# Query projection written transposed, with Wo loads and spare groups placed anew, in an attention and feed-forward kernel on one Trainium2 core

## What is computed

```python
H, D = 32, 32                                   # heads, head size; Hd = 1024; 4 x 512 = 2048 tokens
xn = layernorm(x)
q = (xn @ Wq.T + bq).reshape(B, S, H, D)        # k and v likewise
scores = einsum('bshd,bsgd->bshg', q, k) / sqrt(D)
scores = where(scores > 0.001, scores, -inf)
attn = softmax(scores)
a = einsum('bshg,bsgd->bshd', attn, v).reshape(B, S, Hd) @ Wo.T + bo
f = (silu(xn @ Wg.T) * (xn @ Wu.T)) @ Wd.T      # Wg, Wu: 3584 x 1024, Wd: 1024 x 3584, int4 x scale
out = x + a + f
```

## Time and profile before

| | |
|---|---|
| Median of 3 runs | 2017.5 us (2017.4 to 2018.03) |
| The profiled execution | 2018.38 us, of which the span (first to last instruction) is 2016.6 us |
| PE busy | 1975.8 us, 98% of the span |
| DVE busy | 1613.4 us, 80% |
| ACT busy | 1183.5 us, 59% |
| POOL busy | 1368.3 us, 68% |
| Granted PE clock, mean | 0.996 of full speed |
| DMA engines, mean busy share of the first 13 of 40 slices | 6 to 9 tenths |

### The profile page before, as it was taken

How to read it: one execution, slowest core, us unless ns; L and a number is a source line. 1 busy time by engine, 2 the same in 40 slices (tenths; PEclk the granted TensorE clock), 3 DMA queues, 4 the chain that set the end, 5 groups by cost and what they waited for, 6 DMA issues and landing times.

```text
span 2016.6 us, 36122 instructions
## 1 busy us (share of the span) xinstructions
PE 1975.8 (98%) x10368; PEld 948.6 (47%) x10368; DVE 1613.4 (80%) x1747; ACT 1183.5 (59%) x1934; POOL 1368.3 (68%) x782
## 2 busy tenths in 40 slices
PE   7999999999998999899999999999999999999997
PEld 5555555555554444344444444444444444444444
DVE  6778788887864100799999999999999999999997
ACT  4566666666755212566656666566665666666663
POOL 1455555555562000588889888898888988889898
PEclk9999999999999999999999999999999999999999
DMA  9686776777767552212212122121221212212136
GB/s 304 156 182 161 178 179 157 183 177 165 178 146 204 134 202 63 52 48 57 79 47 50 49 59 77 47 51 48 60 75 47 52 47 62 74 47 52 47 110 250
DMA packets 398869, 219.51 MB, mean 109 GB/s; under 512 B 335984, under 2 KB 372848, under 8 KB 396784
## 3 DMA queue, kind: packets, MB, share of 16 engines
q1 hardware_dynamic: 398832, 219.02, 41.6%
HBM read 96.29 MB, written 41.94 MB: 69 GB/s over the span
## 4 chain that ended last, share of the span: by engine, by line
PE 88%; DVE 6%; issue 3%; POOL 1%; ACT 1%; DMA 0%; DVEq 0%; SPq 0%; ACTq 0%; POOLq 0%
PE banks L710 34%; PE banks L554 24%; PE banks L735 16%; PE banks L652 8%; DVE lower L1211 5%; PE banks L570 1%; PE banks L603 1%; PE banks L587 1%; PE banks L538 1%; POOL acc L1311 1%; DVE wt L1085 0%; PE banks L768 0%; DMA lower<-in_L_attn_Wo_dram 0%; PE banks L633 0%; DMA x_tile<-in_L_attn_x_dram 0%
## 5 line engine op out<-in xcount | busy, mean ns | idle before, releaser
L710 PE MATMUL banks<-xt,lower 128*128 128x512 f16 x3584 | 855.4, 379 | 12.0 <-DVE lower L1211 6.8
L1311 POOL TENSOR_TENSOR acc<-acc,lower 128x1024 f32<-128x1024 f32 x326 | 766.8, 2364 | 130.0 <-ACT lower L1006 130.0
L1006 ACT ACTIVATE lower<-banks,down_scale 128x512 f32<-128x512 f32 x652 | 412.8, 684 | 366.9 <-PE banks L735 287.8
L1211 DVE SCALAR_TENSOR_TENSOR lower<-banks,gate_scale,lower 128x1024 f32<-128x1024 f32 x386 | 472.8, 1277 | 147.8 <-PE banks L710 147.5
L710 PEld LDWEIGHTS banks<-xt,lower 128*128 128x128 f16 x3584 | 344.1, 98 | 454.6 <-DVE lower L1211 67.6
L554 PE MATMUL banks<-wt,xt_tile 128*128 128x512 f16 x2304 | 527.5, 379 | 0.0
L1211 DVE SCALAR_TENSOR_TENSOR lower<-banks,up_scale,lower 128x1024 f32<-128x1024 f32 x388 | 475.4, 1278 | 30.9 <-PE banks L710 27.1
L735 PE MATMUL banks<-lower 128*128 (+1 forms) x1792 | 458.8, 379 | 1.0 <-ACT lower L1006 0.6
L1269 POOL TENSOR_TENSOR stacks<-unit,stacks 128x512 f16<-128x512 f32 x192 | 236.9, 1259 | 276.4 <-ACT stacks L830 276.4
L554 PEld LDWEIGHTS banks<-wt,xt_tile 128*128 (+1 forms) x2304 | 218.0, 98 | 228.3
L735 PEld LDWEIGHTS banks<-lower 128*128 (+1 forms) x1792 | 171.0, 98 | 217.6 <-ACT lower L1006 11.2
(11 more groups left out here) (60 smaller groups left out, 1285.4 us busy)
## 6 DMA issues: line engine op xcount, KB each, us to landing
v_scratch<-stacks SPq DMA_DIRECT2D x16, 1024.0 KB, 3.9
lower<-in_L_ffn_gate_q_dram SPq DMA_DIRECT2D x28, 512.0 KB, 3.7
lower<-in_L_ffn_up_q_dram SPq DMA_DIRECT2D x28, 512.0 KB, 4.4
lower<-in_L_ffn_down_q_dram SPq DMA_DIRECT2D x28, 512.0 KB, 3.9
x_tile<-in_L_attn_x_dram SPq DMA_DIRECT2D x16, 512.0 KB, 3.8
xt_scratch<-xt_tile SPq DMA_DIRECT2D x16, 512.0 KB, 3.2
ctx_scratch<-ctx_parts SPq DMA_DIRECT2D x64, 128.0 KB, 2.1
lower<-ctx_scratch SPq DMA_DIRECT2D x4, 2048.0 KB, 8.5
```

What stands on the lines that cost most here:

```text
L710: last = mm(psum[:, 2 * (slot % 3) + c, :], gu_t[:, mat, g, :], xt[:, (2 * half + c) * CT:(2 * half + c + 1) * CT, part, g, :], start=(par ...
L1006: run(down_tmp[:, buffer, c * BANK:(c + 1) * BANK], psum[:, 6 + c, :], ACT.Copy, scale=scale)\
L1211: v.scalar_tensor_tensor(out=acc_of[:, half, :], in0=gu_pair(slot % 3), scalar=scale[:, :, :].rearrange("p t k -> p (t k)")[:, bass.ds(t * ...
L1311: g.tensor_tensor(acc[:, half, ho, :], acc[:, half, ho, :], down_tmp[:, buffer, :], ALU.add).then_inc(down_added, 1)
```

## The change

Three things are changed.

**Queries.** In units 0 and 1 `project` swaps the operands: a block of Wq is the stationary side and the 128 tokens are the 128 columns that stream. A step of these units is now 24 matmuls of 128 columns (8 blocks of the hidden size times 3 products) instead of 6 of 512, and the queries leave PE already transposed, features on the partitions. The bias becomes one number per partition (`bias_q`). ACT and POOL write one high and one low part, in a strided order, into the new tile `q_parts` (one instruction each per unit instead of two). The turns R0 to R3, their four copies and `ident16` are gone. Instead `move_queries` copies, behind step 11, blocks of 32 rows by 1024 from `q_parts` to their places in `turned[Q]`: four high blocks by DVE, four low blocks by ACT. Behind step 15 `double_queries` has ACT issue two DMAs that copy each 32-row half to the 32 rows beside it. The scores wait for these two DMAs and for the moves. The order of the heads in a block of scores changes with it (`block_of`).

**Wo.** Four blocks of Wo are loaded ahead: blocks 0 and 1 as soon as unit 1 of tile 15 is done, then context 0, then blocks 2 and 3 into the place of `ctx_b` after unit 3. In the opening the first projections wait for as many weight rows as they use.

**Spare groups.** `SPARE` of feed-forward tile 0 takes groups 4, 7, 10, 13, 20, 23, 26, 29 instead of 4, 5, 10, 11, 20, 21, 26, 27.

```diff
-        STEPS = [["S0"], ["S1"], ["S2"], ["S3"], ["X"], [], [], [], [], [], [], [], [], ["R0"],
-                 ["R1"], ["R2"], ["R3", "V0"], ["V1"], [], ["V2"], ["V3"], [], [], []]
+        STEPS = [["S0"], ["S1"], ["S2"], ["S3"], ["X"], [], [], [], [], [], [], [], [], [],
+                 [], [], ["V0"], ["V1"], [], ["V2"], ["V3"], [], [], []]
+        MOVE_AT, DOUBLE_AT = 11, 15
...
+        MOVED_BY = (((HI, 0), (HI, 1), (HI, 2), (HI, 3)), ((LO, 0), (LO, 1), (LO, 2), (LO, 3)))
+        def move_views(part, j):
+            dst = turned[2 * part * DH:(2 * part + 1) * DH, Q, :].rearrange("d (t j o) -> d t j o", j=TG, o=KT)
+            return dst[:, :, j, :], q_parts[j * DH:(j + 1) * DH, part, :].rearrange("d (t o) -> d t o", o=KT)
+        def queries_split(eng, i):
+            eng.wait_ge(unit_lo, i * 6 + (2 * Q + 2))
+            wait_pos(eng, s_done, i * 4)
...
-        SPARE = ((4, 5, 10, 11, 20, 21, 26, 27), (8, 9))
+        SPARE = ((4, 7, 10, 13, 20, 23, 26, 29), (8, 9))
...
+                if u // 2 == Q:
+                    ks, to = range(KT), psum[:, u % 2, (s % 4) * P:(s % 4 + 1) * P]
...
+                        if u // 2 == Q:
+                            last = mm(to, wt[:, Q, wp, k, s * P:(s + 1) * P], xs, start=start, stop=stop)
+                        else:
+                            last = mm(to, xs, wt[:, u // 2, wp, k, (u % 2) * BANK:(u % 2 + 1) * BANK],
+                                      start=start, stop=stop)
...
-                    pe.wait_ge(batch_out[0], j + 1)
-                    pe.wait_ge(batch_out[1], j * 3 + 3)
+                    pe.wait_ge(q_doubled, j * 32 + 32)
+                    pe.wait_ge(q_moved[0], j * 4 + 4)
+                    pe.wait_ge(q_moved[1], j * 4 + 4)
...
+            def double_queries(i):
+                act.wait_ge(q_moved[0], i * 4 + 4)
+                act.wait_ge(q_moved[1], i * 4 + 4)
+                for part in (HI, LO):
+                    at = 2 * part * DH
+                    act.dma_start(turned[at + DH:at + 2 * DH, Q, :], turned[at:at + DH, Q, :]).then_inc(q_doubled, 16)
...
             def load_wo(n):
-                if n >= 2:
+                if n in (4, 5):
+                    sp.wait_ge(wo_turned, 2 * (n - 3))
+                elif n > 5:
                     sp.wait_ge(wo_turned, 2 * (n - 1))
...
+                if ends(i):
+                    sp.wait_ge(unit_done, 6 * (TT - 1) + 2)
+                    load_wo(0)
+                    load_wo(1)
...
+                if ends(i):
+                    sp.wait_ge(ctx_stored, 64 * 2 * CT)
+                    load_context(0)
+                    sp.wait_ge(unit_done, 6 * (TT - 1) + 4)
+                    load_wo(2)
+                    load_wo(3)
```

More of the change, by code:

```diff
@@ L79, in build @@
         ident32 = sb(whole, "ident32", [P, P], F32)
-        ident16 = sb(whole, "ident16", [P, P], F16)
         bias_o = sb(whole, "bias_o", [P, KT], F32)
@@ L170, in build @@
         k_turned = [sem(f"k_turned{k}") for k in range(2)]
+        q_moved = [sem(f"q_moved_{name}") for name in ("dve", "act")]
+        q_doubled = sem("q_doubled")
         v_stored = sem("v_stored")
@@ L192, in build @@
         xt_loaded = sem("xt_loaded")
-        wo_loaded = [sem(f"wo_loaded{k}") for k in range(2)]
+        wo_loaded = [sem(f"wo_loaded{k}") for k in range(KT)]
         wo_turned = sem("wo_turned")
@@ L824, in unit_part @@
                 if u // 2 == Q:
-                    wait_pos(act, batch_done, i * 4)
-                else:
-                    wait_pos(act, k_turned[u % 2] if u // 2 == K else v_stored, i * 16)
+                    wait_pos(act, q_moved[0], i * 4)
+                    run(query_view(u, HI), query_unit(u), ACT.Copy).then_inc(unit_hi, 1)
+                    return
+                wait_pos(act, k_turned[u % 2] if u // 2 == K else v_stored, i * 16)
                 dst, src = stack_view(u, HI), unit_view(u)
@@ L831, in unit_part, with move_queries @@
                 last.then_inc(unit_hi, 1)
-            def batch_copy(j, m):
-                act.wait_ge(batch_done, j * 4 + (m + 1))
-                dst = batch_dest(act, j, m)
-                run(dst, batch_source(m), ACT.Copy).then_inc(batch_out[0], 1)
+            def move_queries(i):
+                queries_split(act, i)
+                for part, j in MOVED_BY[1]:
+                    dst, src = move_views(part, j)
+                    run(dst, src, ACT.Copy).then_inc(q_moved[1], 1)
+            def double_queries(i):
[4 more added lines that the diff above has]
+                    act.dma_start(turned[at + DH:at + 2 * DH, Q, :], turned[at:at + DH, Q, :]).then_inc(q_doubled, 16)
             def scores_out(j, k):
@@ L897, in tile_2 @@
                             x_part(i + 1)
-                        elif kind == "R" and n == 2:
-                            batch_copy(i, n)
                         elif kind == "S":
@@ L912, in tile_2 @@
                         unit_part(i, s // 4)
+                    if s == MOVE_AT and projects(i):
+                        move_queries(i)
+                    if s == DOUBLE_AT and projects(i):
+                        double_queries(i)
             def first_quarter(s):
@@ L965, in spare_copy @@
                 act.wait_ge(gu_done, units_made(t, GU_SLOT[idx]))
-                if g == 5:
+                if t == 0 and g >= 5:
                     dst = spare_b
@@ L1095, in unit_copy, with move_queries @@
                 wait_pos(dve, unit_lo, i * 6 + (u - 1))
-                v.scalar_tensor_tensor(out=unit32[:, u % 2, :], in0=psum[:, u % 2, :], scalar=W_UNSCALE,
-                                       in1=bias_qkv[:, u // 2, (u % 2) * BANK:(u % 2 + 1) * BANK],
-                                       op0=ALU.mult, op1=ALU.add).then_inc(unit_copied, 1)
-            def batch_copy(j, m):
-                dve.wait_ge(batch_done, j * 4 + (m + 1))
-                dst = batch_dest(dve, j, m)
-                v.tensor_copy(dst, batch_source(m)).then_inc(batch_out[1], 1)
+                out, src = unit32[:, u % 2, :], psum[:, u % 2, :]
+                if u // 2 == Q:
+                    out, src = out.rearrange("p (o t) -> p o t", t=P), src.rearrange("p (o t) -> p o t", t=P)
+                    bias = bias_q[:, 4 * u:4 * u + 4].rearrange("p (o t) -> p o t", t=1).broadcast_to((P, 4, P))
+                else:
+                    bias = bias_kv[:, u // 2 - 1, (u % 2) * BANK:(u % 2 + 1) * BANK]
+                v.scalar_tensor_tensor(out=out, in0=src, scalar=W_UNSCALE, in1=bias, op0=ALU.mult, op1=ALU.add)\
+                    .then_inc(unit_copied, 1)
+            def move_queries(i):
+                queries_split(dve, i)
+                for part, j in MOVED_BY[0]:
+                    dst, src = move_views(part, j)
+                    v.tensor_copy(dst, src).then_inc(q_moved[0], 1)
             def over_heads(ap):
@@ L1179, in first_quarter @@
                     unit_copy(0, 5)
[L1180 to L1181 removed]
+                if s == MOVES_0:
+                    move_queries(0)
             def second_x(w):
@@ L1514, in tile_2 @@
                 if not projects(i):
-                    for n in range(3, KT):
+                    for n in range(4, KT):
                         load_wo(n)
```

127 lines of the change are left out of this document (53 added, 74 removed).

## The result

The kernel after takes 2042.8 us (2040.6 to 2046.7), the kernel before 2017.45 us beside it: ratio 1.0127, 95% interval 1.0115 to 1.0139. The forecast was 2003.5. The profiled execution of after takes 2040.63 us, its span 2038.8; the span before was 2016.6, so 22.2 us are to be found.

A forecast was written before the change was run, and what follows sets the result against it. It took PE's own work as the bound. Tiles -5.3, opening -1.0, Wo -5.7 and spare groups -2.0 sum to -14.0 from the profiled 2018.38, 2004.4; the median is 0.9 lower: 2003.5 us, range 1983 to 2016.

The forecast's parts named there:

- V2's wait: In each tile PE waits at V2 for ACT's path to the low part of V0: 1.1 us, bounds 0 and 3.3.
- the doubling: Two DMAs of 256 KB behind step 15, claimed hidden by over 8 us of PE work: no cost in the tile.
- middle case: V2 waits 1.5 to 2.6 us in each tile, around no change: 2010 to 2026 us, chance 0.11.
- three signs of being wrong: V2 starts without idle; PE waits at S0 for K or doubled rows; the gap between short matmuls exceeds 60 ns.
- PE's work: In a tile, 32 turns removed, Q steps 0.32 us dearer at 55.6 ns per short matmul: net -1.46 us, 34.99 a tile.
- Rival 3: Short Q matmuls on PE don't sustain 55.6 ns; at 81 ns the total would be about 2064 us; chance 0.03.
- rival 1: V2 does not wait, so the full gain comes: tile 34.99 us, total 1987 us; chance 0.26.
- POOL's relief: Fewer POOL instructions beside DVE's softmax steps give back 1.5 us of 2.49, so ACT's split of the probabilities starts earlier.
- Moves: ACT's four moves between unit 2 and unit 3, ahead of V0's context, take 3.8 us, bounds 3.6 and 4.2.
- The two issues: ACT's two doubling DMA issues, put beside unit 3 at no cost; 0.74 us if they hold ACT up.
- Rival 2: ACT becomes the bound between unit 2 and V0's context; V2 waits 3.3 us, tile 38.3: 2036 us; chance 0.06.
- Rival 4: DVE's moves hold up POOL's low parts, K's transposes reach S0 2.5 us late, tile up to 38.6: 2041 us; chance 0.04.

The follow-up runs named there:

- no_double: The kernel after with the two doubling DMAs only in the opening, so later tiles score with tile 0's doubled rows: 2028.9 us, ratio 1.0057.
- hi_early: The kernel after with only two moves on ACT, earlier, behind its split of unit 1, and six on DVE; doubling kept: 2040.2 us, ratio 1.0116.
- hi_early_no_double: The kernel after with two early moves on ACT, six on DVE, and the doubling DMAs only in the opening: 2001.9 us, ratio 0.9924.
- dma_dose: The kernel after with twelve moves replacing the doubling, plus two DMAs nobody reads at the doubling's place, bodies 1 to 14: 2076.7 us, ratio 1.0293.
- before_wo: The kernel before with the new Wo loads alone: 2017.56 us, ratio 1.0000.

## Why the prediction was wrong, point by point

**Two terms of the tile failed, and either alone was enough.** The sum had 1.1 us for V2's wait, which made a tile of 36.1, and nothing for the doubling. The wait was 1.93 us, and 0.34 more ahead of V0. That alone takes the kernel out of the range: in no_double, without the doubling, V2 waits 1.86 us, the tile is 37.36 and the time 2028.9. So does the doubling alone: in hi_early, with no move ahead of V0, the tile is 37.82 and the time 2040.2. With both gone the time is 2001.9. A third, smaller part is the price of the Wo loads, below. The prediction's middle case had a wait of 1.5 to 2.6 us in V2 and 2010 to 2026 us: the wait came out in it, and the time passed it by what the doubling and the loads cost. Of the three signs of being wrong that the prediction named, none came in an ordinary tile: V2 did wait, S0 did not, and the short matmuls kept their pace.

**PE's work: right.** 96 short matmuls run from 345.28 to 350.64, 55.8 ns each; 55.6 was forecast. Rival 3 is out, and with it the 81 ns of the Trainium skill ("TensorE: Matmul & The Clock Gate", "Back-to-back issue gap"): the trace disagrees for 96 pairs in a row. With both hindrances gone, bodies 3 to 13 of hi_early_no_double took 35.09 to 35.25 us, where rival 1 had 34.99.

**V2's wait: the mechanism right, three sizes off.** Forecast 1.1 us, measured 1.93, and 0.34 ahead of V0 that I had not seen.
- POOL's relief: 1.5 us forecast, 0.78 measured. ACT's split of the probabilities starts 17.58 us behind S0 (357.04 - 339.46) instead of 18.36 (345.49 - 327.13). The shift fell to 1.23 us and the division from 1.80 to 1.23, but the low part of x grew from 2.17 to 2.56 us beside POOL's one strided instruction (2.4 us here), and the row maximum began 0.4 us later.
- Moves: 4.29 us, not 3.8. Four of 1.07 do not overlap.
- The two issues: from the end of the moves (364.95) to the context of V0 (366.31) ACT takes 1.36 us, for 1.14 us of work: 0.2 that I had put at nothing.

The low part of V0 is out at 367.88 + 1.74 = 369.62, 30.16 us behind S0; the forecast has 355.6 - 327.13 = 28.47. Of these 1.7 us the three terms make 0.72 + 0.49 + 0.2 = 1.4. V2 itself was due 0.9 us later than forecast (369.66 - 1.93 is 28.27 behind S0, 354.5 is 27.37), 0.34 of it the wait ahead of V0, and that hides part. Another 0.2 is in the forecast's reading: 356.00 is V2's weight load, and its first matmul starts at 356.21.

**Doubling: a term put at nothing.** "The DMA engines are 0.72 busy; one more transfer of the size of row 8's first adds under a tenth", and K "hidden, if only just". 0.72 is the mean of a tile. From 352 to 362, where the last of the probabilities' transposes and K's run, the share is 1.04 to 1.10, and a transfer there is paid: 3.2 us of K's issue in after, 4.1 us of the probabilities' in dma_dose. I had the slack of K at about a microsecond and still added bytes in front of it.

**Rivals.** Rival 2 has the place of one of the two causes and 2036 us, near the result, but that is luck: it needed a wait of 3.3 us in V2, and 1.93 came. Rival 4 is near the time (2041) by luck too: POOL's low parts of the probabilities took 0.66 to 0.85 us beside the moves (5.62 us for eight, 5.08 before), while DVE's moves, 0.41 us at best, took up to 0.91. I had weighed there that a copy of DVE shuts POOL out. The Trainium skill, "SBUF — State Buffer", section "Who interferes with whom", says it of whichever of the two issues first, and the other waits. The trace agrees in kind, with DVE as the one that waited: the first move, ahead of POOL's first low part, took 0.41 us, the next, beside it, 0.91.

**Opening: the gain not seen.** S0 of body 1 waited 3.23 us for the doubled rows, not 1. It starts at 72.70, and the three kernels with the old opening have 71.98 to 73.52 in one trace each, so the sign of the 0.7 is not told. Body 1 took 4 us more than the other tiles, which the sum did not have: from S0 to S3 8.1 us instead of 5.4 and from V2 to the next S0 9.1 instead of 7.4, both behind a wait and at a lower granted clock (last section).

**Wo: the saving right, its price missed.** 4.4 us were saved behind S0 of the last body, 5.7 forecast. I did not count that the loads stand ahead of K's transposes on SP; that wait took 3.3 us in before_wo, 2.8 in no_double and, with the doubling, 5.3 in after.

**Spare groups: 2.0 forecast**, about 1.8 measured alone, which the interval does not tell from nothing.

**The range** was built from ACT's uncertainty alone, and no term in it stood for a transfer that is paid for. All upper bounds together (+28, 0, -2.5, 0) would have given 2043, but by a wait of 3.3 us in V2, which did not come.

## What to carry to other kernels

Read a shared resource in the stretch where the new work falls, not as a mean: a DMA share of 0.72 over a tile was 1.1 where the doubling went and 0.00 a few microseconds earlier. Before adding a transfer beside transposes on the critical path, look for a stretch where the DMA engines are idle, or where what runs beside it has slack, or make a copy on an engine that is waiting. When a path has a slack of half a microsecond and a second one has a microsecond, price both; here each by itself was enough to lose the gain, and taking one away alone gave 2.6 or 13.9 of the 40.9 us that both gave.
